# Two routed FFNs around an attention on one core: GpSimd normalises half the tiles, fewer idle products, slots compared in two forms, 28 tiles projected late

## The reference

```
x = x + 0.5 * ffn(layernorm(x))
x = x + attention(layernorm(x))
x = x + 0.5 * ffn(layernorm(x))

def ffn(x):                               # 8 experts, the best one for each token
    probs = softmax(x @ Wr + br); gates = max(probs); idx = argmax(probs)
    xn = normalised x * ln_g + ln_b
    y = relu(xn @ W1[idx] + b1[idx]) @ W2[idx] + b2[idx]     # 128 -> 512 -> 128
    return y * gates

def attention(x):                         # 16 heads of width 8, causal
    q, k, v = heads of x @ Wq.T, x @ Wk.T, x @ Wv.T; q, k = rope(q), rope(k)
    return merge(softmax(causal(q k^T) / sqrt(8)) v) @ Wo.T
```

## Time and profile before

| what | value |
|---|---|
| median of 3 runs | 780.15 (779.5 to 780.86) |
| the profiled execution: time, span | 779.25, 777.5 |
| mean granted TensorE clock | 0.991 |
| busy: PE, DVE, ACT, POOL | 95%, 78%, 65%, 41% of the span |
| first FFN, to the projection's first scales | 0 to 138 |
| projection, its last store issued | 138 to 209 |
| attention | to 650 |
| second FFN | 650 to 777.5 |

### The profile page before, as it was taken

How to read it: one execution, slowest core, us unless ns; L and a number is a source line. 1 busy time by engine, 2 the same in 40 slices (tenths; PEclk the granted TensorE clock), 3 DMA queues, 4 the chain that set the end, 5 groups by cost and what they waited for, 6 DMA issues and landing times. The chain is left out here.

```text
span 777.5 us, 17214 instructions
## 1 busy us (share of the span) xinstructions
PE 737.0 (95%) x5299; PEld 397.5 (51%) x5299; DVE 607.4 (78%) x1927; ACT 505.5 (65%) x1221; POOL 322.6 (41%) x609
## 2 busy tenths in 40 slices
PE   9889999898999999999999999999999998889994
PEld 7378997455433333333333333333333354388894
DVE  5957774399898988888888889888898856956663
ACT  3166662476357887888778877878887781166662
POOL 6177744166522234223333422442233320177753
PEclk9999999999999999999999999999999999999998
DMA  9821212127551442353144314522442010321110
GB/s 284 297 59 51 56 37 92 51 69 194 150 87 28 93 90 57 49 97 83 48 98 96 67 36 100 118 61 44 97 86 59 23 51 26 118 57 50 54 36 28
DMA packets 36654, 63.68 MB, mean 82 GB/s; under 512 B 10456, under 2 KB 22104, under 8 KB 35160
## 3 DMA queue, kind: packets, MB, share of 16 engines
q1 hardware_dynamic: 30472, 53.13, 28.3%
q0 software_dynamic: 4096, 8.69, 4.1%
q10 hardware_dynamic: 2000, 0.80, 0.4%
HBM read 39.12 MB, written 23.09 MB: 80 GB/s over the span
## 5 line engine op out<-in xcount | busy, mean ns | idle before, releaser
L1555 DVE CUSTOM_DVE_ANT_0 cst<-psS,mask_row 128x768 bf16<-128x768 f32 (+7 forms) x512 | 359.7, 754 | 48.9 <-PE psS L1406 46.2
L1518 ACT ACTIVATE prob<-psST 128x512 f32<-128x512 f32 (+3 forms) x750 | 321.5, 494 | 97.7 <-PE psST L1456 59.5
L1471 PE MATMUL a_psO<-prob,vs 128*32 128x512 f32 (+3 forms) x1536 | 159.1, 497 | 0.0
L1678 POOL TENSOR_TENSOR a_gate<-a_zeros 1x1 f32<-1x1 f32 x128 | 23.5, 183 | 265.4 <-ACT prob L1518 264.9
L1456 PE MATMUL psST<-a_qs,ks 75*128 75x512 bf16 (+1 forms) x480 | 126.4, 328 | 0.0
L1406 PE MATMUL psS<-ks,a_qs 72*128 72x512 bf16 (+2 forms) x480 | 114.3, 326 | 0.1
L1456 PEld LDWEIGHTS psST<-a_qs,ks 75*128 75x128 bf16 x480 | 41.6, 97 | 99.0 <-ACT prob L1518 68.6
L811 POOL DMA_INDIRECT tok<-rows,f_there_number x64 | 61.8, 965 | 73.2 <-DVE f_number L510 32.7
L1679 POOL TENSOR_SCALAR_AFFINE_SELECT prob<-prob 128x512 f32<-128x512 f32 x128 | 79.9, 624 | 0.0
L1456 PE MATMUL psST<-qs,ks 75*128 75x512 bf16 (+3 forms) x270 | 72.0, 328 | 0.2
L1406 PE MATMUL psS<-ks,qs 72*128 72x512 bf16 (+3 forms) x288 | 68.8, 327 | 0.7 <-DVE a_rowmax L1555 0.3
(11 more groups left out here) (197 smaller groups left out, 1014.1 us busy)
## 6 DMA issues: line engine op xcount, KB each, us to landing
sums<-p_anT SPq DMA_DIRECT2D x30, 256.0 KB, 4.6
a_qs<-q_split SPq DMA_DIRECT2D x60, 96.0 KB
rows<-tok SPq DMA_DIRECT2D x8, 536.0 KB, 4.8
ks<-k_split SPq DMA_DIRECT2D x32, 128.0 KB
qs<-q_split SPq DMA_DIRECT2D x36, 96.0 KB
q_split<-p_part SPq DMA_DIRECT2D x24, 128.0 KB, 2.4
k_split<-p_part SPq DMA_DIRECT2D x24, 128.0 KB, 2.4
ks<-k_split SPq DMA_DIRECT2D x16, 192.0 KB
```

The source lines that it names most:

```text
L1471: last = nc.tensor.matmul(psO[32 * h:32 * h + 32, c0:c0 + w], vs[r][:, j, h, :], prob[:, u % RING, h, 0:w], start=(j == 0), stop=(u + 1 in ...
L1518: nc.scalar.activation(prob[:, u % RING, h, 0:w], score_buffer(s, u * QH + h)[:, 0:w], ACT.Exp, scale=SCALE).then_inc(exp_done, 1)
L1555: last = nc.vector.tensor_tensor_reduce(out=out[:, a * CH:a * CH + width], in0=ps[:, a * CH:a * CH + width], in1=mask_row[:, S - width:], ...
```

## The change

Five edits, in the order of the program:

1. **Slots compared in two forms.** The table `slot` becomes 8 times as wide (each number repeated 8 times), so that one `tensor_tensor` of 128x1024 compares 8 tiles at once. Tiles 0 to 15 are done by two such instructions, tiles 16 to 31 by the old form. The wide result lies as [part][slot][tile], so a tile's stationary operand for PE has a step of 8 elements. `slot` becomes bf16, and a copy in f32 is kept (`slot32`). The tile's column part (`low`) stands between the two wide compares. The table's transfer grows from 460 to 716 KB.
2. **Idle products.** `FILL` goes from (20, 24) to (16, 13): 16 products fewer after the projection, 44 fewer ahead of it. The second FFN's row of 40 becomes 38, and its row of 5 goes.
3. **Normalisation.** ACT normalises tiles 0 and 1 of a group, POOL tiles 2 and 3, with a semaphore of its own. PE's `turn` waits for both.
4. **28 tiles projected late.** Two more `project` jobs (four tiles) stand around `turn_out` and `turn_back` at the end of the last stage; the second FFN projects four tiles, not eight.
5. The last division counts in `divided`, not in `added`, and stays where it was in the order.

```
-LATE_TILES = 24
+LATE_TILES = 28
-    20, (0, 0, 0, 0, 0, 0, 0, 0), (14, 40), 2, 20, (4, 10), 5)
+    20, (0, 0, 0, 0, 0, 0, 0, 0), (14, 38), 2, 20, (4, 10), 0)
+
+MANY = 2 * TB
-WARM, FILL = 20, (20, 24)
+WARM, FILL = 20, (16, 13)
-for _name, _width in (("before", P), ("slot", P), ("tile", NT * NT), ("column", NT),
+for _name, _width in (("before", P), ("slot", P * TB), ("ramp", P), ("tile", NT * NT), ("column", NT),
-    put("slot", i)
+    put("slot", np.repeat(i, TB))
+    put("ramp", i)
+        many_slots = spare[:, 0:MANY * P].rearrange("p (q k t) -> p q k t", k=P, t=TB)
...
+            def low():
+                dve.wait_ge(tiles_found, 1)
+                nc.vector.tensor_tensor(tile_number[:, :, 1, :], tile_is,
+                                        fixed("column").unsqueeze(2).to_broadcast([P, NT, NT]),
+                                        ALU.mult).then_inc(low_made, 1)
...
-                link(nc.vector.tensor_copy(slot[:, :], place[1][:, :]))
+                link.then(nc.vector.tensor_copy(slot[:, :], place[1][:, :]))
+                link(nc.vector.tensor_copy(slot32[:, :], place[1][:, :]))
...
-                for t in range(1, NT):
-                    nc.vector.tensor_scalar(slot_is[:, t, :], fixed("slot"), slot[:, t:t + 1], None,
+                for q in range(MANY // TB):
+                    if q == 1:
+                        low()
+                    nc.vector.tensor_tensor(many_slots[:, q, :, :],
+                                            slot[:, q * TB:(q + 1) * TB].unsqueeze(1).to_broadcast([P, P, TB]),
+                                            fixed("slot", a=P, b=TB), ALU.is_equal).then_inc(slots_found, TB)
+                for t in range(MANY, NT):
+                    nc.vector.tensor_scalar(slot_is[:, t, :], fixed("ramp"), slot32[:, t:t + 1], None,
                                             ALU.is_equal).then_inc(slots_found, 1)
...
-                last = nc.tensor.matmul(psM, slot_is[:, t, :],
+                last = nc.tensor.matmul(psM, many_slots[:, t // TB, :, t % TB] if t < MANY else slot_is[:, t, :],
...
+    ACT_TILES = 2
...
             pe.wait_ge(normed, g + 1)
+            pe.wait_ge(rest_normed, 16 + g + 1)
...
-            for j in range(CB):
+            for j in range(ACT_TILES):
...
+        def normalise(g, k):
+            pool.wait_ge(scales_ready, 1 if g < NCH else 2)
+            wait(pool, turned, g - 1)
+            for j in range(ACT_TILES, CB):
+                t = g * CB + j
+                last = nc.gpsimd.tensor_scalar(an[k][:, j, :], n.tok[:, t, 0:D], root[:, t:t + 1], offset[:, t:t + 1],
+                                               ALU.mult, ALU.add)
+            last.then_inc(rest_normed, 1)
...
+        for g in range(3):
+            normalise(g, g % 2)
         for g in range(NC8):
             add_pairs(g, g % 2)
+            if g + 3 < NC8:
+                normalise(g + 3, (g + 1) % 2)
             if g >= 1:
                 subtract_mid(g - 1, (g - 1) % 2, 1)
...
-    program[-1] += [("turn_out", NST - 1, 1, 0), ("turn_back", NST - 1, 1, 0)]
+    program[-1] += [("project", NST - 1, LATE_TILES // 2 - 2, 0), ("turn_out", NST - 1, 1, 0),
+                    ("project", NST - 1, LATE_TILES // 2 - 1, 0), ("turn_back", NST - 1, 1, 0)]
...
-                if what == "project" and 2 * arg + 2 == LATE_TILES:
+                if what == "project" and arg == LAST_DIVIDE_AFTER:
...
```

More of the change, by code:

```diff
@@ L313, in ffn @@
         place = [sb(f"place{i}", [P, NT], U32) for i in range(2)]
-        slot, tile = sb("slot", [P, NT]), sb("tile", [P, NT], BF16)
+        slot, slot32, tile = sb("slot", [P, NT], BF16), sb("slot32", [P, NT]), sb("tile", [P, NT], BF16)
         whole = [sb(f"whole{i}", [P, E], U32) for i in range(2)]
@@ L483, in positions @@
                 link(nc.vector.tensor_scalar(place[1][:, :], place[0][:, :], P - 1, None, ALU.bitwise_and))
-                link(nc.vector.tensor_copy(slot[:, :], place[1][:, :]))
-                link(nc.vector.tensor_tensor(tile[:, :], pick[:, :], slot[:, :], ALU.subtract))
+                link.then(nc.vector.tensor_copy(slot[:, :], place[1][:, :]))
+                link(nc.vector.tensor_copy(slot32[:, :], place[1][:, :]))
+                link(nc.vector.tensor_tensor(tile[:, :], pick[:, :], slot32[:, :], ALU.subtract))
                 dve.wait_ge(table_read, 16)
@@ L911, in project @@
     rotated, lo_done, turned_copied, v_copied = n.rotated, n.lo_done, n.turned_copied, n.v_copied
-    x_back = n.x_loaded[0:2]
+    x_back, rest_normed = n.x_loaded[0:2], n.x_loaded[2]
+    ACT_TILES = 2
     split_stored = n.split_stored
@@ L1169, in attention @@
     COPIES = {FIRST: (5, None), MIDDLE: (6, 1), LAST: (6, 2)}
-    INVERT_AFTER, LAST_INVERT_AFTER = (12, 13), 6
+    INVERT_AFTER, LAST_INVERT_AFTER, LAST_DIVIDE_AFTER = (12, 13), 6, LATE_TILES // 2 - 3
     OWN_MASKS = 1
@@ L1604, in divide_last @@
             rows = attended[0:batch_rows(B - 1), ds((B - 1) * S + ch * CH, CH)]
-            nc.vector.tensor_tensor(rows, rows, n.inverse[ch][0:batch_rows(B - 1), :], ALU.mult).then_inc(added, 1)
+            nc.vector.tensor_tensor(rows, rows, n.inverse[ch][0:batch_rows(B - 1), :], ALU.mult).then_inc(divided, 1)
         def invert(s, b, ch):
@@ L1634, in _ @@
         run(stage)
-        dve.wait_ge(added, 1 + LATE_TILES + NCH)
+        dve.wait_ge(added, 1 + LATE_TILES)
+        dve.wait_ge(divided, NCH * B)
     @block.gpsimd
```

## The result

The changed kernel takes 768.86 (median of four), the kernel before 780.47 on the same chip: a ratio of 0.9846, with a 95% interval from 0.9826 to 0.9866. The forecast was 770.4, its range 766.5 to 776. One execution of 784.75, at a mean granted clock of 0.942, lies outside the comparison; its cause is open, for the stall of the last three experiments left 0.977 even in an execution of 787.54.

A forecast was written before the change was run, and what follows sets the result against it. DVE was taken to bound the second FFN's start and the projection's loop, idle products the projection's first turn. Compares -2.2, projection -5.1 and block 2's start -2.4 make -9.7: 769.55 from 779.25, plus 0.9 to the median, 770.4; range 766.5 to 776.

The forecast's parts named there:

- Compares: Slot compares in both FFNs: wide instructions for tiles 0 to 15 save 1.1 each, 2.2 for both.
- the rival with L487's price: Slot compares: a wide compare costs what L487 costs, gain 0.1 not 1.1 each, 772.4; 10 in 100.
- The stepped weight loads: PE's loads for tiles 0 to 15, stepping 16 bytes: taken at the contiguous 96 ns, so no loss.
- The rival of loads at twice the price or five times: PE's stepped loads: at 0.19 each, 772.6, 7 in 100; from 0.46 each, slower than 781.7, 3 in 100.
- Projection's start: Up to rotate 1: shorter fill, shared normalisation and no fall of the clock move it by -6.3.
- Projection's loop: POOL's normalisation slips ahead of DVE's second L953: +0.4 a pass, three passes, +1.2.
- Block 2's start: Attention's end and second FFN's start: two moved project jobs and four fewer tiles there, net -2.4.
- its -2.9: Second FFN's start: adding one group of four tiles, not two, brings DVE to its last group 2.9 sooner.
- a possible 0.8: Block 2's start: if the two moved jobs keep the clock up, 0.8 better; not in the sum.
- The +0.5 for the two pairs: Attention's end: the two added project jobs delay the second turn and copy by 0.5, bounds 0 and 1.4.
- The missing contention: Projection's loop: POOL's normalisations and DVE's two-operand subtractions exclude each other, +1.2 over three passes.

The follow-up runs named there:

- the last three experiments: Changed kernel with a semaphore for each output half, 0.9848; with one store issued late and the old wait, 0.9995; late store with those semaphores, 0.9849.
- experiments 1 and 2: Changed kernel with ScalarE normalising all four tiles again, 0.9877; changed kernel with the fills of before, 0.9908; both against the kernel before.
- Experiment 6: Changed kernel with GpSimd normalising three of a group's four tiles instead of two: ratio 0.9858 to the kernel before.
- experiment 5: Kernel before with eight idle 512-column products added at the attention's end, no tile moved: ratio 0.9985 to the kernel before.
- experiment 4: Changed kernel with the narrow compares of before for all tiles and the narrow table: ratio 0.9898 to the kernel before.
- experiment 3: Changed kernel with 24 tiles projected late and the second FFN's 40 and 5 idle products of before: ratio 0.9876 to the kernel before.
- experiment 2: Changed kernel with the fills of before, 20 and 24 times four idle products: ratio 0.9908 to the kernel before.
- experiment 9: Changed kernel with one store of the attention's output issued behind four stack loads, old wait kept: ratio 0.9995 to the kernel before.
- experiments 4 and 7: Changed kernel with narrow compares and table of before, 0.9898; changed kernel with all 32 tiles compared wide, 0.9855; both against the kernel before.

## Why the prediction was right, step by step

**Compares: right in the sum, with one price wrong.** 1.13 for each FFN against 1.1. The wide compare has a pitch of 0.60 (forecast 0.65), so the rival with L487's price is out. The Trainium skill's page "VectorE: DVE Perf Modes" (the perf-mode tier table) has a bf16 `tensor_tensor` in SBUF at twice the rate of an fp32 one. The estimate that the prediction made from it, 0.69, agrees with the 0.68 measured.

The stepped weight loads were taken at the price of contiguous ones. They take 144 ns, contiguous ones 98, in the changed kernel's rows of L682. That is more than the 109 ns from one product to the next, so by the prediction's reckoning (16 times a load less a product) some 0.56 would have gone in each FFN. Nothing went: the products follow each other every 109 ns through both kinds. That no loss was forecast was right for a reason that did not hold, and in so far luck. The rival of loads at twice the price or five times is out. The Trainium skill's page "SBUF — State Buffer" (Door 1: The DMA port swizzle) says that an access which goes to a new 16-byte line each time pays a penalty. The trace agrees in so far as a stepped load takes 46 ns more; that the lines are the reason no run here shows.

**Projection's start: right.** -6.17 against -6.3, and experiments 1 and 2 split it as the sum did: the fill holds the first turn (4.02), GpSimd's share takes the idle stretch from 2.22, with a fall of the clock behind it, to 1.45, without one (2.66 with the tiles). GpSimd's 0.45 a tile stood against 0.4.

**Projection's loop: the step failed.** "One of them slips in ahead of DVE's second L953: +0.4 a pass" did not happen. VectorE's pair took 2.36 as before, GpSimd's two tiles waited beside it in time that GpSimd had idle, and +1.2 became +0.14. With the tiles it is GpSimd that gives way: its first tile takes 1.40 instead of 0.45, VectorE's subtraction beside it its 0.68. Experiment 6 shows where a loss would have begun.

**Block 2's start: two terms were mis-sized.** -2.4 was forecast, -3.68 measured. The group of tiles that fell away brought its -2.9. The clock, which I had left out of the sum as a possible 0.8, stayed up: the first group reaches VectorE 6.18 behind the last copy (644.90 - 638.72), not 6.94 (652.08 - 645.14), so 0.76 sooner, and the two make up the 3.68. The 1.68 of experiment 5 is larger because two groups wait for slow products there.

The +0.5 for the two pairs came to nothing. It is there in the attention's last product (from 647.28 - 645.14 = 2.14 behind the copy to 2.68), but does not reach block 2's first product, which comes 4.98 behind the copy in both kernels; PE's wait ahead of it shrank from 1.80 to 1.26 by as much. The traces show what sets that product's time: at the end of a block each engine waits for the `DRAIN` of all the others, and GpSimd's is the last, here for the kernel before (first two lines) and the changed one (count, ns min/median/max, first and last start):

```profile
L227 POOLq DRAIN  x1: 6123/6123/6123, 643.7 to 643.7; - x1
L227 DVEq DRAIN  x1: 534/534/534, 648.6 to 648.6; - x1
...
L230 POOLq DRAIN  x1: 6135/6135/6135, 637.3 to 637.3; - x1
L230 DVEq DRAIN  x1: 466/466/466, 642.8 to 642.8; - x1
```

GpSimd's ends 4.7 behind the copy in both, VectorE's 3.96 before and 4.51 now. So the two pairs used room that GpSimd left, and some 0.2 of it remains. Why GpSimd's takes 6.1 no trace shows.

**Given back: not forecast.** The first choice's +0.68 varies like that without the change (experiment 4). The attention's +0.34 does so too: without a stall of 2 or more that stretch took 452.84 to 453.99 in the traces of the changed kernel and its variants, 453.43 and 454.22 in those of the kernel before and experiment 5. The +0.53 at the end does not: 101.39 to 101.61 in the eight traces with wide compares and 28 late tiles, 101.16 and 101.22 without the one or the other (experiments 4 and 3), 101.02 and 101.04 with neither. It goes with the change, and takes back part of what the second FFN's start gained; its cause is open.

The missing contention and block 2's start (2.3 together) outweigh the 1.55 given back: 10.7 less in the trace, where 9.7 was forecast. That the sum came so near is in part luck, as misses of both signs met in it.

## What to carry to other kernels

Price an idle stretch of PE by what it does to the clock behind it, not only by its length: 0.8 less of idle time was worth 1.28 more at the projection, and eight idle products at the attention's end 1.68. Work that is moved to an engine whose idle time lies beside its rival's busy time costs nothing until that room is used up, so measure the room, not the collision. And a wait should count the buffer that it is for: a count over all stores had the copy wait for a store that it did not need, with 0.8 to spare in the changed kernel's trace.

## What I had not expected of the hardware

A stall of 2.1 to 4.4 on PE was followed by a clock of about 0.50 for several us more, and its length did not tell how long. Behind 2.5 in experiment 3 the clock was 0.50 from 388 to 408, of which the last 2:

```profile
406.00:408.00 2.00, 2.00 (x12) 0.56 (x5) 0.00 (x0) 0.68 (x2) 0.30 (x1) 0.50 0.00 0
```

Behind 2.4 in experiment 2 it was 0.50 from 394 to 400. In experiment 9 it was 0.53 from 388 to 392, 0.50 to 396, 0.69 to 400 and then 1.00 behind the stall of 4.4, and 0.54 and 0.61 from 504 to 512 behind the one of 2.1. Stalls of 0.7 and 0.6 in experiments 4 and 7 left it at 1.00.

A store of 256 KB beside a stage's stack loads took 4.0 to 7.8 at one and the same place of the program from one kernel to the next. And GpSimd's tile costs 0.45 alone but 1.40 beside VectorE's second subtraction, which reads two operands from SBUF and keeps its 0.68.
